# Local layers: the MLP norm's mean and variance summed on 32 rows in column quarters, spread by transfers, and the mean subtracted on GpSimd

## The reference

```python
def ffn_layer(x, g, bln, W1, b1, W2, b2):
    mu = x.mean(-1, keepdims=True)
    var = ((x - mu) ** 2).mean(-1, keepdims=True)
    xn = (x - mu) / jnp.sqrt(var + 1e-05) * g + bln
    hg = xn @ W1 + b1
    a, gate = jnp.split(hg, 2, -1)
    return a * jax.nn.gelu(gate, approximate=False) @ W2 + b2
for i in range(DEPTH):     # 6
    x = attn_layer(shift_tokens(x), Wqkv[i], q_scale[i], k_scale[i], Wo[i]) + x
    x = ffn_layer(shift_tokens(x), ln_g[i], ln_b[i], W1[i], b1[i], W2[i], b2[i]) + x
```

## Time and profile before

| what | value |
|---|---|
| time, median of 3 runs | 6622.44 us (6621.18 to 6631.18) |
| the profiled execution: its own time | 6623.76 us |
| the profiled execution: its span | 6622.0 us |
| busy share of the span | PE 91%, DVE 63%, ACT 52%, POOL 34% |
| the local stage | from about 3340 us to the end |

### The profile page before, as it was taken

One profiled execution on the slowest core, in us unless ns is written; L12 is line 12 of the kernel. 1 busy time (PEld: TensorE's weight loads), 2 busy tenths in 40 slices (PEclk: granted clock), 3 DMA queues, 4 the chain that ended last, 5 costly groups with the idle time before them and its releaser, 6 DMA issues. The chain is left out here.

```text
span 6622.0 us, 128662 instructions
## 1 busy us (share of the span) xinstructions
PE 6003.8 (91%) x51745; PEld 3325.1 (50%) x51745; DVE 4160.9 (63%) x6986; ACT 3471.2 (52%) x5688; POOL 2272.1 (34%) x1589
## 2 busy tenths in 40 slices
PE   7999988999777777999769999999999999999998
PEld 3555554444442223766435555555555555555554
DVE  2333333444358886332768888888888888788885
ACT  3343323666434443444536666666666666666664
POOL 0111100222114443000035555555555555555553
PEclk9999987999968888999879999999999999999998
DMA  1000000222200000000011111111111111111111
GB/s 55 1 1 1 1 0 16 52 52 52 62 5 0 0 0 0 1 0 0 1 45 33 33 46 37 33 46 37 33 43 40 33 40 40 33 35 46 37 38 27
DMA packets 184105, 175.14 MB, mean 26 GB/s; under 512 B 24181, under 2 KB 174742, under 8 KB 183318
## 3 DMA queue, kind: packets, MB, share of 16 engines
q1 hardware_dynamic: 183542, 167.27, 10.6%
HBM read 30.88 MB, written 2.10 MB: 5 GB/s over the span
## 5 line engine op out<-in xcount | busy, mean ns | idle before, releaser
L2545 POOL TENSOR_TENSOR local_ssum<-local_sq 128x512 f32<-128x512 f32 x384 | 694.1, 1808 | 2149.4 <-ACT local_sq L2333 2148.9
L2553 POOL TENSOR_TENSOR local_rot<-local_rot,local_inv_all 128x512 f32<-128x512 f32 x768 | 963.3, 1286 | 87.4 <-DMA local_inv_all<-local_inv 86.7
L2154 PE MATMUL banks<-local_y,local_Wqkv 128*128 128x512 f32 x1536 | 823.4, 618 | 64.2 <-ACT local_sq L2333 61.4
L2355 ACT ACTIVATE local_probs<-local_probs,local_npeak 128x1152 f32<-128x1152 f32 x384 | 482.7, 1257 | 355.2 <-DVE local_probs L2459 355.2
L2459 DVE TENSOR_TENSOR local_probs<-banks,band 128x576 f32<-128x576 f32 x768 | 546.0, 752 | 184.7 <-PE banks L2189 179.3
L2439 DVE TENSOR_TENSOR local_rot<-banks,local_rotary_scaled 128x512 f32<-128x512 f32 x768 | 525.2, 684 | 192.1 <-PE banks L2154 186.4
L2333 ACT ACTIVATE local_sq<-banks 128x512 f32<-128x512 f32 x768 | 459.4, 598 | 246.6 <-DVE local_sin L2440 238.3
L2349 ACT COPY local_v<-banks 128x512 f32<-128x512 f32 x384 | 224.8, 585 | 594.6 <-PE banks L2167 594.1
L2446 DVE TENSOR_TENSOR local_rot<-local_rot,local_sin 128x1024 f32<-128x1024 f32 x384 | 504.9, 1315 | 40.8 <-DVE local_sin L2440 0.9
L2189 PEld LDWEIGHTS banks<-local_rot 32*128 32x128 f32 x12288 | 415.4, 185 | 225.2 <-issue 198.6
L2440 DVE TENSOR_TENSOR local_sin<-banks,local_rotary_scaled 128x512 f32<-128x512 f32 x768 | 521.8, 679 | 0.0
(11 more groups left out here) (399 smaller groups left out, 10905.1 us busy)
## 6 DMA issues: line engine op xcount, KB each, us to landing
local_inv_all<-local_inv SPq DMA_DIRECT2D x768, 128.0 KB, 2.7
cosine_inv_all<-cosine_inv SPq DMA_DIRECT2D x256, 128.0 KB, 2.6
local_Wqkv<-in_L_ffn_Wqkv_quads SPq DMA_DIRECT2D x36, 256.0 KB, 2.9
local_Wo<-in_L_ffn_Wo_quads SPq DMA_DIRECT2D x6, 512.0 KB, 4.1
experts_w_W<-in_L_ffn_W SPq DMA_DIRECT2D x1, 2048.0 KB
out<-x SPq DMA_DIRECT2D x8, 256.0 KB, 2.3
local_W<-in_L_ffn_W SPq DMA_DIRECT2D x12, 170.5 KB, 2.3
cosine_w_Wqkv<-in_L_attn_w_kv SPq DMA_DIRECT2D x1, 1024.0 KB
```

What stands on the lines that cost most here:

```text
L2154: pe.matmul(seqs(banks[:, QK_BANK, :]), Wqkv[:, at:at + P], y_group(g), start=True, stop=True).then_inc(qk_projected, 1)
L2355: act.activation(a, a, ACT.Exp, bias=npeak[:, layer:layer + 1], scale=SCALE).then_inc(exped, 1)
L2545: pool.tensor_tensor(ssum[:, n % 2, m, :], sq[:, 0, :], sq[:, 1, :], ALU.add).then_inc(square_summed, 1)
L2553: pool.tensor_tensor(a, a, twice(inv_all[:, n % 2, m, of_seq(s)]), ALU.mult).then_inc(united, 1)
```

## The change

The mean is no longer taken by a matmul on 128 rows. In step 4G + 7 `mean` sums y over the features in four quarters of 128 columns, each onto 32 rows of the bank (four matmuls 128x32, which leave quarter c on rows 32c to 32c + 31). `take_mean` on ACT scales it into a new tile `token_stat` (128x128). `send_mean` on SP issues four transfers, each of which reads 32 rows four times over and writes 128 rows of `yc`. `center_mlp` now stands on POOL, after the second sum of squares of step 4G + 7. In step 4G + 8 the square comes earlier on ACT, `variance` is again four matmuls 128x32 and stands where the centering matmul stood, `root` works on 128x128 and stands ahead of the last square of the step, and `send_rstd` issues four more transfers, for which `scale_mlp` waits. DVE's copy `take_centered` is gone.

```diff
@@ PE
-                def center_mlp(G):
-                    take_x(centered, G + 1)
+                def mean(G):
+                    take_x(mean_taken, G + 1)
                     pe.wait_ge(added, 2 * G + 2)
-                    pe.matmul(seqs(banks[:, X_BANK, :]), center[:], y_group(G % GROUPS), ...).then_inc(centering, 1)
+                    for c in range(GT):
+                        at = c % ST * P
+                        last = pe.matmul(banks[32 * c:32 * c + 32, X_BANK, 0:P], consts["ones"][:, 0:32],
+                                         y[:, 2 * (G % GROUPS) + c // ST, at:at + P], start=True, stop=True)
+                    last.then_inc(y_summed, 1)
...
                     if 1 <= i <= N:
                         norm(i - 1)
+                    if (G := mlp_at(i, 7)) is not None:
+                        mean(G)
                     if (e := within(2 * (i - 2))) is not None:
                         score(e)
@@ ACT
+                def take_mean(G):
+                    act.wait_ge(y_summed, G + 1)
+                    if G:
+                        act.wait_ge(rstd_sent, 64 * G)
+                    act.activation(token_stat[:], banks[:, X_BANK, 0:P], ACT.Copy, scale=1.0 / D).then_inc(mean_taken, 1)
...
+                    act.wait_ge(mean_sent, 64 * (G + 1))
+                    act.activation(token_stat[:], banks[:, X_BANK, 0:P], ACT.Ln, bias=eps[:], scale=1.0 / D).then_inc(var_logged, 1)
@@ DVE
-                def take_centered(G):
-                    dve.wait_ge(centering, G + 1)
-                    dve.tensor_copy(yc[:], banks[:, X_BANK, :]).then_inc(centered, 1)
@@ POOL
+                def center_mlp(G):
+                    pool.wait_ge(mean_sent, 64 * (G + 1))
+                    pool.tensor_tensor(seqs(yc[:]), y_group(G % GROUPS), seqs(yc[:]), ALU.subtract).then_inc(centered, 1)
...
                 def scale_mlp(G):
-                    pool.wait_ge(rstd_done, G + 1)
+                    pool.wait_ge(rstd_sent, 64 * (G + 1))
@@ SP
+                def send_token_stat(into, sent):
+                    for c in range(GT):
+                        rows_c = token_stat[32 * c:32 * c + 32, :]
+                        source = bass.AP(rows_c.tensor, rows_c.offset, [rows_c.ap[0], [0, 4], rows_c.ap[-1]])
+                        sp.dma_start(into[:, c * P:(c + 1) * P], source).then_inc(sent, 16)
```

More of the change, by code:

```diff
@@ L2236, in variance @@
                     pe.wait_ge(mlp_squared, G + 1)
-                    pe.matmul(banks[:, X_BANK, :], consts["ones"], msq[:], start=True, stop=True).then_inc(var_summed, 1)
+                    for c in range(GT):
+                        last = pe.matmul(banks[32 * c:32 * c + 32, X_BANK, 0:P], consts["ones"][:, 0:32], msq[:, c * P:(c + 1) * P],
+                                         start=True, stop=True)
+                    last.then_inc(var_summed, 1)
                 def wide(c, column, signal):
@@ L2302, in _ @@
                     if (G := mlp_at(i, 8)) is not None:
-                        center_mlp(G)
+                        variance(G)
                     if (G := mlp_at(i, 9)) is not None:
@@ L2362, in root @@
                     act.wait_ge(var_summed, G + 1)
-                    act.activation(msq[:], banks[:, X_BANK, :], ACT.Ln, bias=eps[:], scale=1.0 / D).then_inc(var_logged, 1)
+                    act.wait_ge(mean_sent, 64 * (G + 1))
+                    act.activation(token_stat[:], banks[:, X_BANK, 0:P], ACT.Ln, bias=eps[:], scale=1.0 / D).then_inc(var_logged, 1)
                     act.wait_ge(var_logged, G + 1)
-                    act.activation(msq[:], msq[:], ACT.Exp, scale=-0.5).then_inc(rstd_done, 1)
+                    act.activation(token_stat[:], token_stat[:], ACT.Exp, scale=-0.5).then_inc(rstd_done, 1)
                 def make_z(G):
@@ L2393, in _ @@
                         exp(e)
+                    if (G := mlp_at(i, 7)) is not None:
+                        take_mean(G)
+                    if (G := mlp_at(i, 8)) is not None:
+                        square_mlp(G)
                     if i < N:
@@ L2408, in _ @@
                     if (G := mlp_at(i, 8)) is not None:
-                        square_mlp(G)
+                        root(G)
                     if (G := mlp_at(i, 9)) is not None:
@@ L2569, in _ @@
                         sum_squares(2 * i + 1)
+                    if (G := mlp_at(i, 7)) is not None:
+                        center_mlp(G)
             @block.sync
@@ L2580, in send_inverse, with send_mean, send_rstd @@
                         sp.dma_start(inv_all[:, n % 2, c // 2, of_seq(c % 2)], source).then_inc(inv_sent[n % 2], 16)
+                def send_token_stat(into, sent):
+                    for c in range(GT):
+                        rows_c = token_stat[32 * c:32 * c + 32, :]
+                        source = bass.AP(rows_c.tensor, rows_c.offset, [rows_c.ap[0], [0, 4], rows_c.ap[-1]])
+                        sp.dma_start(into[:, c * P:(c + 1) * P], source).then_inc(sent, 16)
+                def send_mean(G):
+                    sp.wait_ge(mean_taken, G + 1)
+                    if G:
+                        sp.wait_ge(z_ready, G)
+                    send_token_stat(yc, mean_sent)
+                def send_rstd(G):
+                    sp.wait_ge(rstd_done, G + 1)
+                    send_token_stat(msq, rstd_sent)
                 def next_weights(i):
@@ L2619, in _ @@
                         send_inverse(i - 1)
+                    if (G := mlp_at(i, 7)) is not None:
+                        send_mean(G)
+                    if (G := mlp_at(i, 8)) is not None:
+                        send_rstd(G)
                     if (G := turn_at(i)) is not None:
```

18 lines of the change are left out of this document (5 added, 13 removed).

## The result

The changed kernel takes 6679.7 us in the median (6677.34 to 6681.86, 4 runs) against 6624.2 for the kernel before, run beside it. The ratio is 1.0081 with a 95% interval of 1.0065 to 1.0097: slower, by 55 us or 0.8%. The forecast was 6696 in 6645 to 6740: inside the range, and 16 us too high.

A forecast was written before the change was run, and what follows sets the result against it. PE, 98% busy, was taken as the bound, but the mean's waits would stall it: 47 x (1.82 - 0.30) + 2 = 73 us on 6623.8, that is 6697, or 6696 against the median; range 6645 to 6740.

The forecast's parts named there:

- The mean's wait for the clamp: Step i mod 4 = 3: the mean behind `norm` waits for DVE's clamp, so the score starts 1.33 us later (1.24 to 1.52).
- The widening's wait for the copy: Step i mod 4 = 3: the first `widen` waits for ACT's copy behind the exponential, +0.49 us (0.2 to 0.6).
- the step's sum: Step i mod 4 = 3: the clamp wait and the copy wait together, +1.82 us a repetition.
- every step of a repetition is the same within hundredths in this trace: Premise for adding up differences of tenths and multiplying them by the repetitions, 47 of 48 groups.
- The step with i mod 4 = 0: Short variance replaces the centering matmul, and the variance matmul's place is freed: -0.30 us for the step (nothing to 0.7).
- Transfers and GpSimd free: Mean and root sends and POOL's MLP work cost nothing, with 2.0 us to spare.
- The last group: Nothing runs beside the second send there, so 2 us are added once (0 to 5).
- PE's freed time: Rival: both PE blocks shrink from 0.96 to 0.38 us and all of it counts, 56 us less, 6567; 8%.
- the stall: Rival: the step 3 delay is given back as DVE and ACT catch up in steps 0 to 2, about 6622; 5%.
- the two new sends: Rival: eight more transfers per group on SP's queue come late and hold up POOL's multiply, 6770 or more; 7%.

The follow-up runs named there:

- Experiments 1: The changed kernel with the mean's four matmuls behind the even score instead of ahead of it: 6629.6 us.
- 9: The kernel before with one wait added: in steps 4G + 7 PE waits behind `norm` until VectorE's clamp is done: 6651.3 us.
- experiment 2: The changed kernel with ACT's copy of the mean ahead of the even exponential, the mean's matmuls still ahead of the score: 6663.3 us.
- experiment 8: The changed kernel with the four variance matmuls issued three times over into the same place: 6675.7 us.
- Experiments 6: The changed kernel with mean behind score, its copy ahead of the exponential, its transfers held until the inverse norms' landed, and root behind `take_den`: 6638.3 us.
- 12: The changed kernel with each send of four transfers issued twice, the second time into a tile nobody reads: 6734.8 us.
- experiment 3: The changed kernel with the mean behind the even score and its ACT copy ahead of the even exponential: 6628.6 us, ratio to before 1.0007.

## Why the prediction was right, and where it was off

- **The mean's wait for the clamp:** forecast +1.33 for the score, measured 1.29, with 0.36 for the mean's block where I had 0.38. Experiments 1 and 9 show that it is this wait.
- **The widening's wait for the copy:** forecast 0.49, measured 0.38; experiment 2 took 0.40 off the step. The copy took 0.26 us instead of 0.275, started 0.09 before the end of the exponential's record, where I had allowed 0.02, and the widening started 0.05 behind it instead of 0.07.
- **The term that was mis-sized** is the step's sum, 47 x 1.82 = 85.5 us; measured 62.5. Of the 23 us, 47 x (1.82 - 1.66) = 7.5 come from the two waits' sizes (1.29 + 0.37 at the odd score, 16.48 - 14.82). The other 15.5 go against the sentence "every step of a repetition is the same within hundredths in this trace". It held for the seventeen repetitions ahead of the one that I read (14.81 to 14.83 us; that one was 14.87), and was false for 23 of the 48: there the step was longer already, behind late transfers, by 14.5 us in sum. The changed kernel has 16.47 to 16.49 in 46 of 48; its second one is 15.48, 1.0 short. The new stall hides the old one: where the step was longer already, it adds less.
- **The step with i mod 4 = 0:** forecast -0.30 a repetition, measured 14.7 / 47 = 0.31. That the two agree so well is in part luck. In the plain steps it is 0.39 (16.42 to 16.03), and the mean comes to 0.31 because the first two steps grew a little, and of the five in which the layer changes four grew by 0.40 to 0.45 and one fell by 1.15. The -0.30 was in any case taken from within wide bounds (0 to 0.7), and not added up from rows. That the removed PE time would give little is shown by the idle times of 0.30 and 0.53 and by experiment 8.
- **Transfers and GpSimd free:** forecast 2.0 us of room, measured 2.25, and 2.3 us in sum in the steps with 1. A send took 4.1 us from its first issue (5117.64) to POOL's start (5121.76), where I had taken the 4.8 of the inverse norms; and the 5017.45 from which I counted the root stands in no row, the square in that place starts at 5017.42. Experiments 6 and 12 are past the edge of that room, the changed kernel on this side of it.
- **The last group:** 3.6 us instead of 2, inside the bounds of 0 to 5.
- **The rivals:** PE's freed time does not count (8); the stall was not given back elsewhere, but partly laid over older ones (9); the two new sends were not late. The old one, of the inverse norms, was, in both kernels, and none of my rivals had it.

The parts add up: 62.5 - 14.7 + 2.3 + 3.6 + 0.1 = 53.8.

## What to carry to other kernels

Before a matmul is put behind another user of the same bank, look when that bank is emptied, and by which engine: four matmuls that take 0.36 us together cost 1.29 because the reader had two instructions to do first. A chain of waits that runs along one engine says that it is the bound, not that its blocks can be cut one by one: ask for each what stands ready behind it. And before a per-repetition price is multiplied, list the lengths of all repetitions: a stall costs less where the step already waits for something else.

## What the runs showed of the hardware that was not expected

The same four transfers of the inverse norms landed 4.5 us after the first issue in one repetition and 5.9 in another of the same execution, with nothing else of the kernel in the queue, and the step grew from 14.82 to 15.83 with them. In most of the late ones the queue itself was held longer, up to 3.74 us instead of 2.49; but in three it was free after 2.48 to 2.50, and the landing was at 5.4 to 5.5 all the same. What makes them slow was not found; holding back the transfers behind them did not make them fewer.

VectorE's add of two SBUF operands takes 1.23 us in the median and up to 2.30 beside GpSimd (kernel before, 384 adds). GpSimd's sum of squares takes 1.26 to 1.30 us in the nine cases in which no such add runs beside it, and 1.74 to 2.28 in all others. From experiment 3, VectorE and GpSimd:

```profile
5072.52 1.90 DVE L2462 TENSOR_TENSOR local_rot<-local_rot,local_sin 128x1024 f32<-128x1024 f32 x1
```

```profile
5068.36 4.97 POOL L2563 TENSOR_TENSOR local_rot<-local_rot,local_inv_all 128x512 f32<-128x512 f32 x4 [1.08 <-DMA local_inv_all<-local_inv]
5073.30 2.25 POOL L2555 TENSOR_TENSOR local_ssum<-local_sq 128x512 f32<-128x512 f32 x1
```

The Trainium skill, GPSIMD Engine Reference, Specifications, says that GpSimd shares its SBUF interface with VectorE and contends with instructions that have two SBUF inputs; the 1.90 here against 1.23 agrees. GpSimd's sum took 2.25 there. Four 128x32 matmuls of 128 columns hold PE for 0.36 us and twelve of them for 0.80; ACT's instructions on 128 columns take 0.26 (copy), 0.35 (Ln) and 0.31 (Exp).
